# Products of the identity with a bias table: the whole array against two halves of its rows

## The chip, the cores and the metric

The kernel runs on one core of one Trainium2 chip. The metric is the device time of one execution in microseconds (us). Several executions are timed, and one more is profiled; its span and every row below come from that one.

## The reference

A block of attention and a gated feed-forward part, each with a layer norm and a residual, on x of 8 x 256 tokens by 128 features:

```
x = x + layernorm(attention(layernorm(x)))
x = x + layernorm(ffn(x normalised))

attention, 16 heads of 8 features, batches of 256 tokens:
  scores = q k^T / sqrt(8) + rel_bias[clip(i - j + 128, 0, 256)]
  out    = softmax(scores) v, projected by W_out

ffn: h = silu(x w1^T s1) * (x w2^T s2); two layers of 512 x 512 with exact gelu; one of 512 to 128
```

The bias of a head depends only on i - j. So for one head a table of 128 partitions by 384 columns, in which partition p holds the head's bias vector shifted by p, holds all 256 x 256 values: the bias of the second block of 128 rows is the same table, read from another column on.

## The kernel before, in words

**The parts.** The first 31 us load x, normalise it, make the rows of q and k of batch 0 and the maxima of batch 0's scores. Then the attention runs over batches b = 0 to 7, and in each over pairs s = 0 to 7 of two heads (the two heads of a pair are called its halves). From 194 us on the feed-forward part runs, which the change doesn't touch.

**A pair on TensorE.** q and k of a head stand in 33 rows (four parts of 8 that carry the precision, and one row for the maximum or for ones), the first head of a pair on partitions 0 to 32, the second on 64 to 96. In each step of the main loop PE (TensorE) issues, in this order:
- `scores(b, s)`, L1278: 4 products of 33 rows, into one of three two-bank PSUM tiles `place`. The bias was copied into the tile before, by ScalarE (L1023) or VectorE (L699), from the table `raw`; ScalarE then takes the exp (L1016).
- `max_scores(b + 1, s)`, L1244: 4 products of 33 rows, the scores of the next batch, by which their maxima are found.
- `max_bias(b + 1, s)`, L1252: the bias is added to them, by 2 products of the 128 x 128 identity `identr` with 512 columns of `table_hi`, one for each head. VectorE then takes the maxima (L692).
- for pair 7 (`BY_PE`) also `score_bias(b, s)`, L1289: 4 products of the same kind, with `table_hi` and `table_lo`, in place of the copy.
- behind that one other thing: `weighted` (L1304, 16 products with v, four at a time in different columns of the array) behind even pairs, transposes or the output's projection (L1315, L1322, L1261, L1328, L1335) behind odd ones.

A tile `place` is used in turn by scores and by maxima, so exp, products, maxima and bias copy of different pairs wait for each other in a ring of three.

**The tables.** `raw` holds all 16 heads on 128 partitions, 384 columns each, loaded by `load_table` on SP's queue, one pair (384 KB) at a time, among the loads of x. GpSimd copies it into `table_hi` in the rounded format that TensorE takes at full speed (`table_high`, L525), and makes the remainder `table_lo` for pair 7 (L545).

**SP's queue.** The order of SP's transfers is written out by hand: x and tables; then the parts of q and k of unit 1 to DRAM (`store_parts(1)`); a wait until these have landed; eight row loads of batch 1 (`row_dmas(1, ...)`); `load_x(4)`; and then the negated maxima of batch 0, which go from `mrow` into the 33rd rows of q (`send_mrow(sp, 0, 0)`). PE's first `scores(0, 0)` waits for this last transfer, and its first `max_scores(1, 0)` for the row loads.

Of the kernel before, what the change touches and what calls it, by code (L numbers as in the profile page):

```python
# [4 lines left out]
F32 = mybir.dt.float32  # L5
# [9 lines left out]
P = 128  # L15
# [5 lines left out]
REL = 2 * MAX_REL + 1  # L21
WIN = P + S
EXT = WIN + P - 1
CH = 512
NCH = TOK // CH
TPC = CH // P
# [31 lines left out]
BY_PE = (7,)  # L58
BY_DVE = (2, 5)
LAST_BY_DVE = (1, 2, 4, 5, 6)  # L60
LOW_AT_SLOT = {2 * s + k: 2 * i + k for i, s in enumerate(BY_PE) for k in range(2)}


def windows(ap, start, step, count, width):

    return bass.AP(tensor=ap.tensor, offset=ap.offset + start, ap=[list(ap.ap[0]), [step, count], [1, width]])
# [20 lines left out]
def build(nc, x, wq, wk, wv, bqk, brows, bv, wo, bo, ext, w1, s1, w2, s2, h1, h1s, h2, h2s, w3, w3s,  # L87
          ident_in, out):
    ctx = ExitStack()
    with ctx:  # L90
        def sb(name, shape, dt=F32):
            return ctx.enter_context(nc.sbuf_tensor(name, shape, dt))

        def sem(name):
            return ctx.enter_context(nc.semaphore(name))

        ident = sb("ident", [P, P])
        identr = sb("identr", [P, P], F32R)
        wq_sb = sb("wq_sb", [P, D])
        wk_sb = sb("wk_sb", [P, D])  # L100
        wv_sb = sb("wv_sb", [P, D])
# [34 lines left out]
        taken = [qk_parts[0][:, n, :, 0:S] for n in range(2)]  # L136

        raw = sb("raw", [P, H, WIN])
        hi_at, lo_at = 0, H * WIN
        rows_at = lo_at + 2 * len(BY_PE) * WIN  # L140
        room = sb("room", [P, max(rows_at + 4 * PAIRS * S, 2 * NK * CH * SLOTS)], F32R)
        table_hi = room[:, hi_at:lo_at].rearrange("p (h c) -> p h c", h=H)
        table_lo = room[:, lo_at:rows_at].rearrange("p (h c) -> p h c", h=2 * len(BY_PE))
        q_rows = room[:, rows_at:rows_at + 2 * PAIRS * S].rearrange("p (a h n) -> p a h n", a=2, h=PAIRS)
        k_rows = room[:, rows_at + 2 * PAIRS * S:rows_at + 4 * PAIRS * S].rearrange(
            "p (a h n) -> p a h n", a=2, h=PAIRS)
# [55 lines left out]
        def max_tile(i):  # L202
            return place[1 + i % 2 if i < PAIRS else i % 3]

        def score_tile(i):
            return place[i % 3]
# [30 lines left out]
        taken_set = sem("taken_set")  # L237
        row_less = sem("row_less")
        rows_set = sem("rows_set")
        table_hi_pool = sem("table_hi_pool")  # L240
        table_lo_set = sem("table_lo_set")
        dve_order = sem("dve_order")
# [121 lines left out]
        def wait_score_place(eng, i):  # L364

            if i == 0:
                eng.wait_ge(rows_set, 2 * PAIRS)
            elif i == 1:
                eng.wait_ge(ms_read, PAIRS - 1)
            elif i + SHARED < B * PAIRS:  # L370
                eng.wait_ge(ms_read, i + SHARED + 1)
            else:
                eng.wait_ge(exp_done, i - 2)

        def spread_weights(copy, i, halves=range(2)):

            weights = (wq_sb, wk_sb)[i][:, :]
            for half in halves:
# [2 lines left out]
                to = row_w[:, i, :, 64 * half:64 * half + KROWS].rearrange("p s (a d) -> p s a d", a=PARTS)  # L381
                copy(to, src).then_inc(row_w_set[i], 1)

        def load_table(eng, s):
            eng.dma_start(raw[:, 2 * s:2 * s + 2, :],
                          bass.AP(tensor=ext.tensor, offset=2 * s * EXT,
                                  ap=[[1, P], [EXT, 2], [1, WIN]])).then_inc(raw_in[s], 16)
# [9 lines left out]
        def _(sp):  # L397
# [5 lines left out]
            load_x(0)  # L403
            sp.dma_start(ident[:, :], ident_in).then_inc(ident_loaded, 16)
            load_x(1)
            load_table(sp, 0)
            load_x(2)
            load_table(sp, 1)
            load_table(sp, 2)
            sp.wait_ge(ones_set, 2)  # L410
            for half in range(2):
                to = 64 * half + KROWS
                for rows, src in ((q_rows, zeros), (k_rows, ones)):
                    sp.dma_start(rows[to:to + 1, 1, :, :].bitcast(F32), src[0:PAIRS, :].bitcast(F32)).then_inc(extra_in, 16)
            load_table(sp, 3)
            load_table(sp, 4)
            load_x(3)
            for s in range(5, PAIRS):
                load_table(sp, s)

            def store_twice(dram, first, step, src, done):
                plane, row = dram.ap[0][0], dram.ap[1][0]
# [6 lines left out]
            def store_parts(u):  # L429

                first, tiles = UNITS[u]
                tok = slice(first * P, (first + tiles) * P)
                for i, dram in enumerate((q_dram, k_dram)):
                    sp.wait_ge(qk_hi_set, (u - 1) * 2 + i + 1)
                    hi = qk_hi[u][:, i, :].bitcast(F32)
                    if i == 0:
                        sp.dma_start(dram[0, :, tok], hi).then_inc(parts_out[u], 16)
                    else:
                        store_twice(dram[:, :, tok], 0, 2, hi, parts_out[u])
                    sp.wait_ge(qk_lo_set, (u - 1) * 2 + i + 1)  # L440
                    sp.dma_start(dram[1, :, tok], qk_lo[u][:, i, :].bitcast(F32)).then_inc(parts_out[u], 16)
# [22 lines left out]
                row_dmas(b, r * RPAIRS, RPAIRS, rows_in[r][b % 2])  # L464

            store_parts(1)
            sp.wait_ge(parts_out[1], PARTS_OUT)
            row_dmas(1, 0, PAIRS, second_rows_in)
            load_x(4)
# [4 lines left out]
            for b in range(B):  # L474
                send_mrow(sp, b, 1)
                if b == 1:
                    for dst, src in ((hs[:, 0, :], s1), (hs[:, 1, :], s2), (hs[:, 2, :], h1s), (hs[:, 3, :], h2s),
                                     (w3s_sb[:, :], w3s)):
                        sp.dma_start(dst, src).then_inc(scales_in, 16)
                if 1 <= b <= len(matrices):  # L480
                    at, src = matrices[b - 1]
                    sp.dma_start(w_lo[:, at:at + src.shape[-1]], src).then_inc(ffn_w_in[b - 1], 16)
                if b + 2 < B:
                    sp.wait_ge(st_ready, b * PAIRS + RPAIRS)
                    load_rows(b + 2, 0)
                if b == 0:
                    for dst, src in ((wo_sb[:, :], wo), (bo_bc[:, :], bo.broadcast_to((P, D)))):
                        sp.dma_start(dst, src).then_inc(out_w_in, 16)
                    store_parts(3)
                if b + 1 < B:  # L490
                    send_mrow(sp, b + 1, 0)
                if b == 3:
                    store_parts(4)
                if b + 2 < B:
                    sp.wait_ge(st_ready, b * PAIRS + PAIRS)
                    load_rows(b + 2, 1)
# [9 lines left out]
        def _(pool):  # L506
# [14 lines left out]
                inv_std(u + 1, UNITS[u][1], UNITS[u][0])  # L521

            def table_high(s):
                pool.wait_ge(raw_in[s], 16)
                nc.gpsimd.tensor_copy(table_hi[:, 2 * s:2 * s + 2, :],  # L525
                                      raw[:, 2 * s:2 * s + 2, :]).then_inc(table_hi_pool, 1)

            x_inv_std(0)
            pool.wait_ge(qk_w_in[1], 16)
# [10 lines left out]
            pool.wait_ge(xn_set, 4)  # L540
            table_high(6)
            table_high(7)
            for i, s in enumerate(BY_PE):
                pool.wait_ge(table_hi_pool, s + 1)
                nc.gpsimd.tensor_tensor(table_lo[:, 2 * i:2 * i + 2, :], raw[:, 2 * s:2 * s + 2, :],  # L545
                                        table_hi[:, 2 * s:2 * s + 2, :].bitcast(F32),
                                        ALU.subtract).then_inc(table_lo_set, 1)

            x_inv_std(4)
# [60 lines left out]
        def _(dve):  # L610
# [71 lines left out]
            x_normalize(1)  # L682
            dve.wait_ge(qk_w_in[2], 16)
            nc.vector.tensor_scalar(bq_sb[:, 0:1], bq_sb[:, 0:1], scale, None, ALU.mult).then_inc(bq_scaled, 1)
            nc.vector.tensor_copy(identr[:, :], ident[:, :]).then_inc(identr_set, 1)
            x_moments(2)
            q_and_k_low(1, 0)
            q_and_k_low(1, 1)
# [7 lines left out]

            def write_bias(i):
                wait_score_place(dve, i)
                nc.vector.tensor_copy(score_tile(i)[:, :, :].rearrange("p k (j n) -> p k j n", j=2),  # L699
                                      pair_windows(raw[:, :, :], i % PAIRS)).then_inc(bias_set_dve, 1)  # L700

# [232 lines left out]
        def _(act):  # L934
# [85 lines left out]
            def write_bias(i):  # L1020

                wait_score_place(act, i)
                nc.scalar.copy(score_tile(i)[:, :, :].rearrange("p k (j n) -> p k j n", j=2),  # L1023
                               pair_windows(raw[:, :, :], i % PAIRS)).then_inc(bias_set, 1)

# [138 lines left out]
        def _(pe):  # L1164
# [65 lines left out]
            def max_scores(b, s):  # L1230
# [11 lines left out]
                for it in range(TPB):  # L1242
                    for half in range(2):
                        mm(max_tile(b * PAIRS + s)[:, half, it * S:(it + 1) * S],  # L1244
                           rows(q_rows, b, half, s)[:, it * P:(it + 1) * P], rows(k_rows, b, half, s),
                           start=(it == 0), stop=False, skip_group_check=True)

            def max_bias(b, s):
                if b == 0:
                    pe.wait_ge(table_hi_pool, s + 1)  # L1250
                for half in range(2):
                    last = mm(max_tile(b * PAIRS + s)[:, half, :], identr[:, :],  # L1252
                              windows(table_hi[:, 2 * s + half, :], 0, P, 2, S),
                              start=False, stop=True, skip_group_check=True)
                last.then_inc(ms_ready, 1)

            def maxima_T(b, r):
# [26 lines left out]
            def score_bias(b, s):  # L1284
                if b == 0:
                    pe.wait_ge(table_lo_set, BY_PE.index(s) + 1)
                for half in range(2):
                    for part in (table_hi[:, 2 * s + half, :], table_lo[:, LOW_AT_SLOT[2 * s + half], :]):
                        last = mm(score_tile(b * PAIRS + s)[:, half, :], identr[:, :], windows(part, 0, P, 2, S),  # L1289
                                  start=False, stop=True, skip_group_check=True)  # L1290
                last.then_inc(st_ready, 1)

            def weighted(b, g):
# [41 lines left out]
                    last = nc.tensor.transpose(misc[:, it * P:(it + 1) * P], z[:, it, :], ident[:, :])  # L1335
                last.then_inc(zT_ready, 1)

            pe.wait_ge(identr_set, 1)
            for s in range(PAIRS):
                if s + 1 < PAIRS:  # L1340
                    row_lows(s + 1)
# [320 lines left out]
```

## Time and profile before

| | |
|---|---|
| median of 3 runs | 291.06 us (290.31 to 291.15) |
| the profiled execution, its own time | 290.61 us |
| its span | 288.8 us |
| mean granted clock of TensorE | 0.992 |
| attention part | 31 to 194 us of the span |

The span runs from the first to the last instruction, and the time of an execution is 1.8 us longer. In the chain of waits each piece is followed back to what released it. Of products of TensorE the profile gives start and a modelled end; they overlap, so it is the distance between starts that tells the pace.

### The profile page before, as it was taken

Reading aid. Unit: us, or ns where it says so; the run is one execution under the profiler, and the core shown is the slowest. Engines: PE = TensorE matmul, PEld = TensorE weight load, DVE = VectorE, ACT = ScalarE, POOL = GpSimd, SP = SyncE. Lnnn points to the kernel's source line nnn. Section 1 sums busy time; section 2 is a strip of 40 time slices with the busy share of each in tenths; the row PEclk is TensorE's granted clock in tenths of the full one; section 3 lists DMA queues with packets and bytes.
Section 4 is the critical chain, followed back from the end, with each engine's and each line's share of the span. In section 5 each row is a group of like instructions: output and inputs, shape, how many; then the busy total and the mean of one; then the engine's idle time right before and its main releaser. Section 6 shows DMA issues by size and latency. Waiting matters only on the chain.

```text
span 288.8 us, 5174 instructions
## 1 busy us (share of the span) xinstructions
PE 267.7 (93%) x1875; PEld 180.7 (63%) x1875; DVE 212.5 (74%) x442; ACT 205.2 (71%) x316; POOL 102.5 (35%) x107
## 2 busy tenths in 40 slices
PE   7899989899999999999999998999999999999980
PEld 7656646555555555556555554557888888888860
DVE  4576977889789789789788888857654853673675
ACT  2677777785876776785886886767459976896750
POOL 6716000101702603923974985117640202400111
PEclk9999999999999999999999999999999999999996
DMA  6979505322221262560221200000000000010012
GB/s 159 339 231 142 184 5 183 129 65 90 64 84 41 74 194 103 179 210 21 75 78 36 78 0 3 1 3 1 0 2 0 0 0 2 0 36 2 2 36 77
DMA packets 21356, 21.17 MB, mean 73 GB/s; under 512 B 3664, under 2 KB 18768, under 8 KB 21072
## 3 DMA queue, kind: packets, MB, share of 16 engines
q1 hardware_dynamic: 20464, 20.53, 24.4%
q10 hardware_dynamic: 864, 0.27, 0.4%
q8 instruction: 17, 0.28, 0.4%
q14 instruction: 11, 0.09, 0.1%
HBM read 14.90 MB, written 5.64 MB: 71 GB/s over the span
## 4 chain that ended last, share of the span: by engine, by line
PE 68%; DVE 16%; ACT 8%; issue 5%; DMA 1%; POOL 1%; ACTq 0%; POOLq 0%; DVEq 0%
PE place L1449 11%; PE place L1450 11%; PE place L1252 10%; PE pv L1304 7%; DVE mx L692 6%; PE place L1244 5%; ACT ring L1016 4%; PE place L1278 4%; DVE place L699 3%; PE place L1203 2%; PE misc L1315 2%; PE place L1289 2%; PE misc L1182 2%; PE pv L1450 2%; PE pv L1449 2%
## 5 line engine op out<-in xcount | busy, mean ns | idle before, releaser
L692 DVE TENSOR_REDUCE mx<-place 128x4 f32<-128x1024 f32 x64 | 78.3, 1223 | 16.2 <-PE place L1252 14.9
L517 POOL TENSOR_TENSOR rstd<-mv,mhalf 128x2 f32<-128x2 f32 (+1 forms) x26 | 20.9, 806 | 145.8 <-DVE mv L624 145.8
L1016 ACT ACTIVATE ring<-place 128x1024 f32<-128x1024 f32 x64 | 65.7, 1028 | 6.4 <-PE place L1289 3.1
L1252 PE MATMUL place<-room,identr 128*128 128x512 f32 x128 | 47.0, 448 | 0.0
L1023 ACT COPY place<-raw 128x1024 f32<-128x1024 f32 x37 | 37.8, 1024 | 11.7 <-DVE mx L692 11.7
L1449 PE MATMUL place<-room,w_hi 128*128 128x512 f32 (+1 forms) x116 | 44.7, 387 | 0.7 <-DVE room L825 0.7
L1450 PE MATMUL place<-room,w_hi 128*128 128x512 f32 (+1 forms) x116 | 44.1, 383 | 0.0
L1304 PE MATMUL pv<-ring,vx 128*9 128x256 f32 x512 | 33.6, 380 | 0.4 <-ACT ring L1016 0.4
L825 DVE TENSOR_TENSOR room<-ring,room 128x512 fp32r<-128x512 f32 x32 | 21.3, 690 | 17.1 <-ACT room L1104 17.1
L1244 PE MATMUL place<-room 33*128 33x256 f32 x256 | 28.4, 298 | 4.9 <-ACT ring L1016 4.8
L1278 PE MATMUL place<-room 33*128 33x256 f32 x256 | 31.7, 328 | 1.4 <-DVE place L699 1.1
L1278 PEld LDWEIGHTS place<-room 33*128 33x128 f32 x256 | 19.0, 185 | 15.7 <-issue 12.5
L1028 ACT COPY oT<-pv 128x256 f32<-128x256 f32 x32 | 11.8, 370 | 23.2 <-PE pv L1304 23.1
L1244 PEld LDWEIGHTS place<-room 33*128 33x128 f32 x256 | 19.8, 185 | 12.3 <-issue 9.0
L1449 PEld LDWEIGHTS place<-room,w_hi 128*128 128x128 f32 x116 | 21.8, 188 | 5.1 <-DVE room L825 0.9
L1252 PEld LDWEIGHTS place<-room,identr 128*128 128x128 f32 x128 | 19.1, 188 | 8.6
L1450 PEld LDWEIGHTS place<-room,w_hi 128*128 128x128 f32 x116 | 21.8, 188 | 4.1
L699 DVE COPY place<-raw 128x1024 f32<-128x1024 f32 x19 | 23.2, 1225 | 0.6
L1102 ACT ACTIVATE ring<-place,hs 128x512 f32<-128x512 f32 x27 | 18.5, 685 | 5.1 <-PE place L1450 5.1
L1304 PEld LDWEIGHTS pv<-ring,vx 128*9 128x9 f32 x512 | 10.9, 90 | 17.8 <-issue 10.5
L837 DVE SCALAR_TENSOR_TENSOR ring<-place,hs,raw 128x512 f32<-128x512 f32 x16 | 12.0, 750 | 11.9 <-ACT raw L1081 11.6
L1104 ACT CAST room<-ring 128x512 fp32r<-128x512 f32 x32 | 19.9, 621 | 1.0
(141 smaller groups left out, 434.4 us busy)
## 6 DMA issues: line engine op xcount, KB each, us to landing
raw<-ext SPq DMA_DIRECT2D x8, 384.0 KB, 6.8
room<-q_parts SPq DMA_DIRECT2D x48, 64.0 KB
room<-k_parts SPq DMA_DIRECT2D x48, 64.0 KB
w_lo<-h SPq DMA_DIRECT2D x2, 1024.0 KB, 5.6
q_parts<-w_hi SPq DMA_DIRECT2D x4, 256.0 KB, 3.0
k_parts<-w_hi SPq DMA_DIRECT2D x2, 512.0 KB, 3.4
xs<-x SPq DMA_DIRECT2D x3, 256.0 KB, 6.1
w_lo<-w SPq DMA_DIRECT2D x3, 256.0 KB, 2.8
```

Source lines behind the costliest of these rows:

```text
L517: nc.gpsimd.tensor_tensor(rstd[:, at:at + width], mv[:, at:at + width, 1], mhalf[:, 0:width], ALU.pow).then_inc(rstd_set, 1)
L692: nc.vector.tensor_reduce(mx[:, s // RPAIRS, :, :, s % RPAIRS].rearrange("p i k -> p k i"), max_tile(b * PAIRS + s)[:, :, :].rearrange("p ...
L699: nc.vector.tensor_copy(score_tile(i)[:, :, :].rearrange("p k (j n) -> p k j n", j=2), pair_windows(raw[:, :, :], i % PAIRS)).then_inc(bia ...
L825: nc.vector.tensor_tensor(lo, act_f[:, half[c], k, :], hi.bitcast(F32), ALU.subtract).then_inc((a1_lo_set, a2_lo_set)[i], 1)
L1016: nc.scalar.activation(probs[:, s % PRING, :, :, :].rearrange("p k j n -> p (k j n)"), score_tile(b * PAIRS + s)[:, :, :].rearrange("p k n ...
L1023: nc.scalar.copy(score_tile(i)[:, :, :].rearrange("p k (j n) -> p k j n", j=2), pair_windows(raw[:, :, :], i % PAIRS)).then_inc(bias_set, 1)
L1244: mm(max_tile(b * PAIRS + s)[:, half, it * S:(it + 1) * S], rows(q_rows, b, half, s)[:, it * P:(it + 1) * P], rows(k_rows, b, half, s), st ...
L1252: last = mm(max_tile(b * PAIRS + s)[:, half, :], identr[:, :], windows(table_hi[:, 2 * s + half, :], 0, P, 2, S), start=False, stop=True, ...
L1278: last = mm(tile[:, half, j * S:(j + 1) * S], rows(k_rows, b, half, s)[:, j * P:(j + 1) * P], rows(q_rows, b, half, s), start=(s in BY_PE ...
L1304: last = mm(pv[32 * r:32 * r + VC, 0:S], vx[:, b * TPB + j, 4 * g + r, :], probs[:, (2 * g + r // 2) % PRING, r % 2, j, :], start=(j == 0) ...
L1449: mm(o, w, hi, start=first, stop=False)
L1450: done = mm(o, w, lo, start=False, stop=last and exact)
```

## The change

A head's table is held on 64 partitions in place of 128, with 448 columns in place of 384: the first head of a pair on partitions 0 to 63, the second on 64 to 127, as the rows of q and k are. A product of the identity then takes 64 rows of the array. Output rows 0 to 63 of a block come from the table at column 0, output rows 64 to 127 from column 64. For the first the weights are [I, 0], for the second [0, I], both read from one tile `ident_wide` of 192 columns, 0 I 0. Per pair `max_bias` now has 4 products (two column blocks times two heads), and `score_bias` 8.

The half tables are loaded first, in place of the whole ones, into space of `w_lo` (`raw_halves`), 16 transfers of 112 KB. The whole tables `raw`, which the bias copies still read, are loaded by SP behind `store_parts(1)`. ScalarE and VectorE wait for them in `write_bias`. SP waits for `table_hi` and `table_lo` ahead of the weight load at b = 1, whose place is that of the half tables.

```diff
+HP = P // 2
+TWIN = WIN + HP
...
+        def load_halves(eng, s):
+
+            for half in range(2):
+                eng.dma_start(raw_halves[half * HP:(half + 1) * HP, s, :],
+                              bass.AP(tensor=ext.tensor, offset=(2 * s + half) * EXT,
+                                      ap=[[1, HP], [1, TWIN]])).then_inc(table_in[s], 16)
...
-            load_table(sp, 0)
+            load_halves(sp, 0)
             load_x(2)
-            load_table(sp, 1)
-            load_table(sp, 2)
+            load_halves(sp, 1)
+            load_halves(sp, 2)
...
-            load_table(sp, 3)
-            load_table(sp, 4)
+            load_halves(sp, 3)
+            load_halves(sp, 4)
             load_x(3)
             for s in range(5, PAIRS):
-                load_table(sp, s)
+                load_halves(sp, s)
...
             store_parts(1)
+            for s in range(PAIRS):
+                load_table(sp, s)
             sp.wait_ge(parts_out[1], PARTS_OUT)
             row_dmas(1, 0, PAIRS, second_rows_in)
             load_x(4)
...
             def table_high(s):
-                pool.wait_ge(raw_in[s], 16)
-                nc.gpsimd.tensor_copy(table_hi[:, 2 * s:2 * s + 2, :],
-                                      raw[:, 2 * s:2 * s + 2, :]).then_inc(table_hi_pool, 1)
+                pool.wait_ge(table_in[s], 32)
+                nc.gpsimd.tensor_copy(table_hi[:, s, :], raw_halves[:, s, :]).then_inc(table_hi_pool, 1)
...
-            nc.vector.tensor_copy(identr[:, :], ident[:, :]).then_inc(identr_set, 1)
+            dve.wait_ge(blank_set, 1)
+            nc.vector.tensor_copy(ident_wide[:, 0:2 * HP], blank[:, :]).then_inc(identr_set, 1)
+            nc.vector.tensor_copy(ident_wide[:, 2 * HP:3 * HP], blank[:, 0:HP]).then_inc(identr_set, 1)
+            dve.wait_ge(identr_set, 1)
+            for half in range(2):
+                at = half * HP
+                nc.vector.tensor_copy(ident_wide[at:at + HP, HP:2 * HP],
+                                      ident[at:at + HP, at:at + HP]).then_inc(identr_set, 1)
...
             def write_bias(i):
                 wait_score_place(dve, i)
+                dve.wait_ge(raw_in[i % PAIRS], 16)
...
+            def bias_product(tile, table, s, block, half):
+
+                at = half * HP
+                return mm(tile[:, half, :], ident_wide[at:at + HP, HP - block * HP:3 * HP - block * HP],
+                          windows(table[at:at + HP, s, :], block * HP, P, 2, S), start=False, stop=True,
+                          skip_group_check=True)
+
             def max_bias(b, s):
                 if b == 0:
                     pe.wait_ge(table_hi_pool, s + 1)
-                for half in range(2):
-                    last = mm(max_tile(b * PAIRS + s)[:, half, :], identr[:, :],
-                              windows(table_hi[:, 2 * s + half, :], 0, P, 2, S),
-                              start=False, stop=True, skip_group_check=True)
+                for block in range(2):
+                    for half in range(2):
+                        last = bias_product(max_tile(b * PAIRS + s), table_hi, s, block, half)
                 last.then_inc(ms_ready, 1)
```

## Rows read from the trace of the kernel before

**Rows 1.** The page: busy time by engine; transfers in 40 equal slices.

```profile
PE 267.7 (93%) x1875; PEld 180.7 (63%) x1875; DVE 212.5 (74%) x442; ACT 205.2 (71%) x316; POOL 102.5 (35%) x107
...
GB/s 159 339 231 142 184 5 183 129 65 90 64 84 41 74 194 103 179 210 21 75 78 36 78 0 3 1 3 1 0 2 0 0 0 2 0 36 2 2 36 77
```

**Rows 2.** The page: the chain that ended last, by engine and by line.

```profile
PE 68%; DVE 16%; ACT 8%; issue 5%; DMA 1%; POOL 1%; ACTq 0%; POOLq 0%; DVEq 0%
PE place L1449 11%; PE place L1450 11%; PE place L1252 10%; PE pv L1304 7%; DVE mx L692 6%; PE place L1244 5%; ACT ring L1016 4%; PE place L1278 4%; DVE place L699 3%; PE place L1203 2%; PE misc L1315 2%; PE place L1289 2%; PE misc L1182 2%; PE pv L1450 2%; PE pv L1449 2%
```

**Rows 3.** The chain of waits in time, 83 to 126 us: start, us, what.

```profile
94.00 0.95 PE place L1289 x4
...
99.28 0.66 PE place L1252 x2
99.94 0.44 PE misc L1315 x4
...
102.69 0.59 PE misc L1315 x4
...
103.95 0.68 PE place L1252 x2
```

**Rows 4.** Busy time by engine, PEclk, DMA share and GB/s, a batch.

```profile
82.90:104.00 21.10, 20.02 (x171) 11.58 (x172) 17.80 (x32) 15.50 (x23) 6.10 (x6) 1.00 0.27 74
```

**Rows 5.** The chain of waits, 142 to 176 us, shares by line.

```profile
by line: DVE mx L692 21.2%; ACT ring L1016 13.6%; issue 11.5%; PE pv L1304 8.7%; PE place L1252 8.6%; DVE stats L616 5.9%; ACT place L1023 5.6%; PE place L1244 5.1%; PE misc L1328 3.9%; DVE y_and_z L627 3.1%; DVE mv L620 3.0%; DVE y_and_z L
```

**Rows 6.** PE's instructions in order of time, narrow windows: start, us, what.

```profile
103.43 0.28 PE L1278 MATMUL place<-room 33*128 33x256 f32 x2
...
103.67 0.28 PE L1244 MATMUL place<-room 33*128 33x256 f32 x2
103.88 0.50 PE L1252 MATMUL place<-room,identr 128*128 128x512 f32 x1
...
106.25 0.40 PE L1252 MATMUL place<-room,identr 128*128 128x512 f32 x1
106.58 0.41 PE L1304 MATMUL pv<-ring,vx 128*9 128x256 f32 x4
```

**Rows 7.** The same of the first part: VectorE, then weight loads.

```profile
9.55 0.21 DVE L685 CAST identr<-ident 128x128 fp32r<-128x128 f32 x1
...
13.09 0.88 DVE L647 SCALAR_TENSOR_TENSOR z_parts<-place,bq_sb,z_parts 128x256 fp32r<-128x256 f32 x2 [1.93 <-ACT z_parts L954]
...
20.27 0.19 PEld L1210 LDWEIGHTS place<-z_parts,minus_ident 128*128 128x128 f32 x1 [0.45 <-ACT z_parts L967]
```

**Rows 8.** The same, SP's queue: issue time and its length.

```profile
8.84 1.76 SPq L385 DMA_DIRECT2D raw<-ext  x3
...
14.46 0.49 SPq L441 DMA_DIRECT2D k_parts<-z_parts  x1
...
22.86 1.69 SPq L401 DMA_DIRECT2D xs<-x  x1
```

**Rows 9.** Busy time of stretches; the last two columns are DMA share and GB/s.

```profile
14.00:16.00 2.00, 1.99 (x10) 1.20 (x10) 0.65 (x1) 1.39 (x4) 1.00 (x2) 1.00 1.06 370
...
18.00:20.00 2.00, 2.00 (x11) 1.26 (x10) 1.40 (x2) 1.64 (x4) 0.00 (x0) 1.00 0.12 40
...
22.00:28.00 6.00, 6.00 (x33) 4.05 (x32) 4.32 (x13) 4.50 (x11) 3.70 (x4) 1.00 1.17 138
```

**Rows 10.** DMA issues at 22.0 to 22.5, then at 22.8 us: KB, us to landing.

```profile
room<-k_parts SPq DMA_DIRECT2D x2, 128.0 KB, 6.7
...
xs<-x SPq DMA_DIRECT2D x1, 256.0 KB, 7.1
```

**Rows 11.** PE's instructions in order of time, 32 to 35 us.

```profile
33.30 0.51 PE L1278 MATMUL place<-room 33*128 33x256 f32 x4
```

**Rows 12.** The last PE work; then busy time and, third from the end, PEclk.

```profile
280.79 0.78 PE L1542 MATMUL place<-ident,xT 128*128 128x128 f32 x4 [0.42 <-ACT xT L1118]
...
284.00:286.00 2.00, 0.00 (x0) 0.00 (x0) 1.58 (x5) 0.00 (x0) 0.20 (x1) 0.58 0.24 71
```

More of the change, by code:

```diff
@@ L60 @@
 LAST_BY_DVE = (1, 2, 4, 5, 6)
-LOW_AT_SLOT = {2 * s + k: 2 * i + k for i, s in enumerate(BY_PE) for k in range(2)}
+LOW_PAIRS = BY_PE
 def windows(ap, start, step, count, width):
@@ L97, in build @@
         ident = sb("ident", [P, P])
-        identr = sb("identr", [P, P], F32R)
         wq_sb = sb("wq_sb", [P, D])
@@ L138, in build @@
         raw = sb("raw", [P, H, WIN])
[L139 to L143, printed above, removed]
+        hi_at, lo_at = 0, PAIRS * TWIN
+        rows_at = lo_at + len(LOW_PAIRS) * TWIN
+        ident_at = rows_at + 4 * PAIRS * S
+        room = sb("room", [P, max(ident_at + 3 * HP, 2 * NK * CH * SLOTS)], F32R)
+        raw_halves = w_lo[:, 2 * PAIRS * P:2 * PAIRS * P + PAIRS * TWIN].rearrange("p (s c) -> p s c", s=PAIRS)
+        table_hi = room[:, hi_at:lo_at].rearrange("p (s c) -> p s c", s=PAIRS)
+        table_lo = room[:, lo_at:rows_at].rearrange("p (s c) -> p s c", s=len(LOW_PAIRS)) if LOW_PAIRS else None
+        ident_wide = room[:, ident_at:ident_at + 3 * HP]
         q_rows = room[:, rows_at:rows_at + 2 * PAIRS * S].rearrange("p (a h n) -> p a h n", a=2, h=PAIRS)
@@ L239, in build @@
         rows_set = sem("rows_set")
+        table_in = [sem(f"table_in{s}") for s in range(PAIRS)]
         table_hi_pool = sem("table_hi_pool")
@@ L479, in _ @@
                         sp.dma_start(dst, src).then_inc(scales_in, 16)
+                if b == 1:
+                    sp.wait_ge(table_hi_pool, PAIRS)
+                    sp.wait_ge(table_lo_set, len(LOW_PAIRS))
                 if 1 <= b <= len(matrices):
@@ L542, in _ @@
             table_high(7)
-            for i, s in enumerate(BY_PE):
+            for i, s in enumerate(LOW_PAIRS):
                 pool.wait_ge(table_hi_pool, s + 1)
-                nc.gpsimd.tensor_tensor(table_lo[:, 2 * i:2 * i + 2, :], raw[:, 2 * s:2 * s + 2, :],
-                                        table_hi[:, 2 * s:2 * s + 2, :].bitcast(F32),
+                nc.gpsimd.tensor_tensor(table_lo[:, i, :], raw_halves[:, s, :], table_hi[:, s, :].bitcast(F32),
                                         ALU.subtract).then_inc(table_lo_set, 1)
@@ L1022, in write_bias @@
                 wait_score_place(act, i)
+                act.wait_ge(raw_in[i % PAIRS], 16)
                 nc.scalar.copy(score_tile(i)[:, :, :].rearrange("p k (j n) -> p k j n", j=2),
@@ L1286, in score_bias @@
                     pe.wait_ge(table_lo_set, BY_PE.index(s) + 1)
[L1287 to L1290, printed above, removed]
+                for table, at in ((table_hi, s), (table_lo, LOW_PAIRS.index(s))):
+                    for block in range(2):
+                        for half in range(2):
+                            last = bias_product(score_tile(b * PAIRS + s), table, at, block, half)
                 last.then_inc(st_ready, 1)
@@ L1336, in norm_T @@
                 last.then_inc(zT_ready, 1)
-            pe.wait_ge(identr_set, 1)
+            pe.wait_ge(identr_set, 4)
             for s in range(PAIRS):
```

## The prediction

> **What bounds the kernel now.** I read the page's busy shares first. TensorE (PE) is busy 93% of the span, VectorE 74%, ScalarE 71%, and the core's transfers are dense only in the first slices [rows 1]. The chain that ended last is 68% PE and 16% VectorE, and the products of the identity with the table, L1252, hold 10% of it [rows 2]. One batch of the attention part, read from the chain in order of time (82.9 to 104 us), is a nearly closed row of PE work: scores L1278, scores for the maxima L1244, table product L1252, then a product or transpose [rows 3]. So a saving in PE's sequence is worth its face value there, as long as VectorE (17.8 us busy of that batch's 21.1) and ScalarE (15.5) don't take over [rows 4]. From 142 us on, long stretches of the chain are VectorE and ScalarE [rows 5]. The FFN part, from 194 us, is not touched.
>
> **The edit on PE.** max_bias goes from 2 products of 128 rows and 512 columns to 4 of 64 rows and 512 columns, score_bias from 4 to 8. Do two of the new ones run at once, on the two halves of the rows? The score products answer: they use partitions 0 to 32 and 64 to 96, and from their pair at 103.43 to the next but one at 103.67 it is two steps of 0.12 us, and both products of a pair lie inside the same 0.28 us [rows 6]. A pair of 512 columns should then go at the pace of one now, 0.23 us (an L1289 product, 0.95 us for four [rows 3]). Two pairs cost what two products cost: 0.46 us. The streaming time neither gains nor loses. The other end, no overlap, costs 2 x 0.23 us for each of 64 pairs: +29 us.
>
> What goes is the step from half-row products to full-row products. The last L1244 pair starts at 103.67 and needs 0.12 us; L1252 starts only at 103.88, and its first product takes 0.50 us where a second takes 0.40, since it waits 0.10 us for its weights [rows 6]. 103.88 + 0.10 - 103.79 = 0.19, call it 0.20 us for each table product. In the new form its weights can load under the running score products, as those of L1244 do under L1278.
>
> The page "TensorEngine Tiling (Array Packing)" of the Trainium skill, section Key Properties, says that changing the tiling mode drains TensorE. The gap before L1252 agrees. By the same rule the drain returns where a full-row transpose follows the table product, so by it the 6 places counted at 0.05 us below would fall to 0 and the sum to 6.4 us.
>
> The rows say how much returns. Four L1315 transposes cost 0.44 us in the chain behind L1252 but 0.59 behind the pv products, which use the array in another shape [rows 3]: 0.15 us comes back, 0.05 us is left. Behind a table product followed by pv products there is a change of shape already now (L1304 starts 0.33 us after the last L1252 product, whose columns need 0.23 [rows 6]), so nothing comes back: 0.20. Where VectorE, or ScalarE by way of L1289, is released by the product, its end is what counts: 0.20.
>
> In the batch of rows 3 that is 3 to pv, 1 to L1289, 1 to VectorE (the last) at 0.20, and 1 to L1315 at 0.05: 1.05 us. Over the chain from 31 to 190 us I count 32 places at 0.20 and 6 at 0.05 (batches as in rows 3 three times; from 142 us only five): 6.4 + 0.3 = 6.7 us. From it I take 0.7 off for VectorE, which would be 89% busy in a batch of 20.0 us. **6.0 us** saved; bounds 3 (every place where VectorE or ScalarE is next lost) and 7.
>
> **Edits at nothing.** Ahead of 31 us PE waits for ScalarE in each pair, 0.45 us ahead of L1210 [rows 7]: the product's 0.2 us is hidden there. GpSimd's table copies shrink from 768 to 448 columns, and GpSimd has 1% of the chain now [rows 2], so they can only be earlier. VectorE's 0.21 us cast of the identity becomes four copies, at most 4 x 0.21, that is 0.6 us more ahead of an idle time of 1.93 us [rows 7]; without that cover it would be 0.6 us. The new waits on raw_in in write_bias cost nothing if the tables land ahead of the first scores at 33.3 us; behind them ScalarE's and VectorE's queues would hold the first exp and maxima. The wait ahead of the weight load at b = 1 is long met.
>
> **The DMA queue is the price.** SP issues 16 half loads for 8 whole ones: 8 x 0.47 = 3.8 us more, so the last goes out at 14.4 instead of 10.6, and store_parts(1) starts 1.3 us late, ending at 16.2 instead of 14.95 [rows 8]. The bytes there fall (8 x 384 KB to 16 x 112 KB). Then the 8 whole tables, 3.15 MB, are issued, 8 x 0.49 = 3.9 us, to 20.1. The stores, issued from 14.4 to 16.2 into a queue that the smaller halves have left, have landed by then, so row_dmas(1), load_x(4) and send_mrow(0,0) are all issued behind the tables. With tables in it the full queue moves 370 GB/s at most [rows 9], 339 in a whole slice [rows 1]; I take 350: 3.15 / 0.35 = 9.0 us. I allow 2 us from the first issue to the first bytes (in rows 8 and 9, from the last stores at 14.46 and the idle slice behind them, it is not more than some 4), so they hold the engines from 18.2 to 27.2. Now that time is idle at 18 to 20, and the row loads run at 138 GB/s with the engines full (share 1.17) from 20.0 on; the last, issued at 22.4, lands at 22.4 + 6.7 = 29.1, load_x(4) at 22.86 + 7.1 = 30.0 [rows 8 to 10]. That is 9.1 to 10 us of work, moved behind the tables: 27.2 + 9.1 to 10 = 36.3 to 37.2. The mrow copy follows. The first scores(0,0) waits for it, and starts now at 33.3 [rows 11]; behind it on PE stand max_scores(1,0) and with it VectorE's next maxima. A stall of 3.0 to 3.9 us; I take **3.5**. Lower bound 0 (rows at the tables' rate: 27.2 + 1.31 / 0.35 = 31); upper bound: tables at the row loads' 138 GB/s, 23 us, a landing near 51 and a stall of 17. The rows with table loads in them are the 339 to 370, so I stay near it. That nothing overtakes is read from load_x(4), which lands 0.9 us behind the row load ahead of it though it was issued into the same crowd. What is late next, mrow(0,1), is needed four pairs later and is not in danger.
>
> **Sum.** -6.0 + 3.5 = -2.5 us on the profiled execution: 290.61 - 2.5 = 288.1 (span 288.8 to 286.3, 1.8 us around it). The median of the runs is 0.45 above the profiled one: 291.06 - 2.5 = 288.5 us.
>
> **Rivals.**
> A. The clock falls in the stall. PE would be idle 3.5 us with nothing to do. At the end of the kernel the last PE work starts at 280.79 and ends near 281.6, and the granted clock of 284 to 286 is 0.58, which puts the fall to half near 284.3 [rows 12]: 2.7 us after it. Against: gaps there were frequent before that too. If the slow stretch lasts some 4 us and PE is two thirds of the chain, it loses about 1.5: 290.0. The page "TensorE: Matmul & The Clock Gate" (Part 1) of the Trainium skill says that idleness puts the clock to half; it is the same case, and it gives 290.0 too.
> B. No stall: the tables and the rows overlap, or mrow gets in ahead. For: the engines are nearly idle at 18 to 20. Against: share above 1 at only 138 GB/s [rows 9]. 291.06 - 6.0 = 285.0.
> C. Gain given back: each 0.2 us on PE turns into a wait for VectorE's maxima or ScalarE's bias copy (VectorE is 84% busy in rows 4 and leads in rows 5). 3 us saved, 3.5 lost: 291.5, no change.
> D. Slower: the tables go at 230 GB/s (the mean of a slice with mixed loads [rows 1]) or worse; 13.7 us, the mrow copy lands at 41.5, stall 8.2: 291.06 - 6.0 + 8.2 = 293.3. It decides from a landing at 39.3 on. For: everything is one queue. Against: rows 9.
> E. The halves don't overlap at 512 columns: +29 - 6 + 3.5, near 318. Against: rows 6.
>
> **Chances.** Forecast 0.43 (own range 287.3 to 289.8), A 0.20, B 0.12, C 0.10, D 0.12, E 0.03. Range 284.8 to 292.5: E, most of D and the edge of B are left out. A change under 0.3% (0.9 us) can't be told from none. Faster (below 290.2): 0.41 + 0.11 of A + 0.12 of B = 0.64. Same: 0.02 + 0.07 of A + 0.07 of C = 0.16. Slower: 0.20.
>
> **What would show it.** Right: LDWEIGHTS of the table product start while L1244's products run, its first product starts 0.12 us after the last of them, two of its products in the same time, pv starting about 0.2 us sooner; transposes behind it cost 0.15 more; batches of 20.1 instead of 21.1 us. SP's table loads at 16 to 20 us, DMA full to 37, PE idle 33 to 37 for a DMA into room. Wrong: products in single file, batches of 21 us, no idle PE at 33 us, or a clock below 1.00 behind it.

## The result

The changed kernel takes 293.91 us (median of 6 runs, 292.66 to 294.81), against 290.96 us before (6 runs): a ratio of 1.0099, 95% interval 1.0082 to 1.0117. Forecast were 288.5 us, in a range of 284.8 to 292.5. The kernel is slower, by 2.95 us, and the time lies outside the range.

The profiled execution took 293.98 us, its span is 292.2. The page shows two things that it doesn't show before: PE is busy less (263.7 us against 267.7), and the granted clock has a hole in slices 6 and 7 of 40, counted from 1.

```profile
PE 263.7 (90%) x2035; PEld 177.0 (61%) x2035; DVE 212.8 (73%) x445; ACT 205.2 (70%) x316; POOL 100.0 (34%) x107
...
PEclk9999956999999999999999999999999999999996
...
GB/s 175 144 234 363 196 183 3 130 172 75 85 74 101 11 76 221 190 114 174 47 92 48 76 0 3 3 2 0 2 0 0 0 2 0 0 40 0 0 36 76
...
PE 58%; DVE 16%; SPq 9%; ACT 7%; issue 6%; DMA 3%; POOL 0%; ACTq 0%; DVEq 0%
```

The dense transfers have moved from slice 2 to slice 4 against [rows 1], and SP's queue and a DMA hold 12% of a chain in which they had 1% [rows 2]. The waits of PE name the DMA:

```profile
PE place L1313 <- DMA room<-mrow: 6.3, 2, 6.0
PE place L1273 <- ACT ring L1044: 4.3, 12, 0.4
```

PE in order of time, around the first scores(0,0) (now L1313; L1273 are the scores for the maxima, L1280 all products of the identity):

```profile
31.76 1.16 PE L1217 MATMUL pv<-wv_sb,ring 128*128 128x128 f32 x8
38.88 0.80 PE L1313 MATMUL place<-room 33*128 33x256 f32 x4 [5.96 <-DMA room<-mrow]
39.48 0.63 PE L1273 MATMUL place<-room 33*128 33x256 f32 x4
39.91 1.05 PE L1280 MATMUL place<-room 64*128 64x512 f32 x4
```

scores(0,0) starts at 38.88, not at 33.30 [rows 11]. It takes 0.80 us, not 0.51, at a granted clock of 0.50 in place of 1.00. The busy times in stretches show when (third column from the end is the clock):

```profile
32.00:34.00 2.00, 0.92 (x8) 0.73 (x7) 2.00 (x3) 1.42 (x2) 0.00 (x0) 1.00 1.15 191
34.00:36.00 2.00, 0.00 (x0) 0.00 (x0) 0.27 (x1) 0.00 (x0) 0.00 (x0) 0.80 1.19 191
36.00:38.00 2.00, 0.00 (x0) 0.00 (x0) 0.00 (x0) 0.00 (x0) 0.00 (x0) 0.50 1.08 322
...
46.00:48.00 2.00, 2.00 (x20) 0.44 (x16) 1.23 (x1) 1.02 (x2) 0.00 (x0) 0.50 0.00 0
48.00:50.00 2.00, 2.00 (x12) 0.89 (x10) 0.00 (x0) 0.28 (x1) 0.00 (x0) 0.78 0.00 0
```

PE ends its work at 32.9. If the granted clock is either full or half, as wherever it holds for a whole stretch here, 0.80 over 34 to 36 puts the fall at 35.2, and 0.78 over 48 to 50 the rise at 48.9, ten microseconds after PE took up work again.

Behind that hole the kernel is as forecast. A batch takes 20.1 us where it took 21.1 [rows 4], with VectorE 17.70 us busy of it:

```profile
90.20:110.30 20.10, 19.03 (x191) 10.82 (x192) 17.70 (x33) 15.53 (x23) 6.10 (x6) 1.00 0.21 59
```

One pair of it, from its scores to the transposes behind the table product, PE in order of time (the last line is the next pair's first products):

```profile
104.58 0.50 PE L1313 MATMUL place<-room 33*128 33x256 f32 x4
104.92 0.40 PE L1273 MATMUL place<-room 33*128 33x256 f32 x4
105.16 0.63 PE L1280 MATMUL place<-room 64*128 64x512 f32 x4
105.72 0.66 PE L1350 MATMUL misc<-ident,oT 128*128 128x128 f32 x4
106.30 0.39 PE L1313 MATMUL place<-room 33*128 33x256 f32 x2
```

The same place in the kernel before:

```profile
103.55 0.40 PE L1244 MATMUL place<-room 33*128 33x256 f32 x4
103.88 0.74 PE L1252 MATMUL place<-room,identr 128*128 128x512 f32 x2
```

L1280 starts 0.24 us after L1273, where L1252 started 0.33 after L1244 and then waited 0.10 for its weights [rows 6]. Four products take 0.63 us, where two took 0.74. The weights of L1280 now load while L1273 still runs (first line), and in the chain of waits a table product takes 0.47 us (0.66 to 0.68 in [rows 3]) and the four transposes behind it 0.59:

```profile
105.04 0.31 PEld L1280 LDWEIGHTS place<-room 64*128 64x128 f32 x4
...
105.32 0.47 PE place L1280 x4
105.79 0.59 PE misc L1350 x4
```

### The profile page after: what moved, and what is told of

Same layout as the page of the kernel before. It is cut to its first block, busy times and chain, and to the rows that moved or that the text cites. A ratio compares the mean times of both kernels' runs of the same rounds, so it can differ in the third digit from the quotient of the medians.

```text
span 292.2 us, 5568 instructions
## 1 busy us (share of the span) xinstructions
PE 263.7 (90%) x2035; PEld 177.0 (61%) x2035; DVE 212.8 (73%) x445; ACT 205.2 (70%) x316; POOL 100.0 (34%) x107
## 4 chain that ended last, share of the span: by engine, by line
PE 58%; DVE 16%; SPq 9%; ACT 7%; issue 6%; DMA 3%; POOL 0%; ACTq 0%; DVEq 0%
PE place L1484 11%; PE place L1485 10%; PE place L1280 8%; PE pv L1339 7%; DVE mx L719 7%; PE place L1313 4%; PE place L1273 4%; ACT ring L1044 4%; DVE place L727 4%; SPq L396 3%; DMA room<-mrow 3%; PE misc L1350 2%; SPq L468 2%; PE misc L1211 2%; PE pv L1485 2%
## 5 line engine op out<-in xcount | busy, mean ns | idle before, releaser
L1280 PE MATMUL place<-room 64*128 64x512 f32 x320 | 49.6, 401 | 0.0
L1313 PE MATMUL place<-room 33*128 33x256 f32 x256 | 32.6, 336 | 7.0 <-DMA room<-mrow 6.3
L1339 PE MATMUL pv<-ring,vx 128*9 128x256 f32 x512 | 34.5, 388 | 0.5 <-ACT ring L1044 0.5
L853 DVE TENSOR_TENSOR room<-ring,room 128x512 fp32r<-128x512 f32 x32 | 21.3, 689 | 17.1 <-ACT room L1133 17.1
L1273 PE MATMUL place<-room 33*128 33x256 f32 x256 | 29.2, 305 | 4.6 <-ACT ring L1044 4.3
L1313 PEld LDWEIGHTS place<-room 33*128 33x128 f32 x256 | 19.6, 190 | 21.9 <-issue 13.2
L1273 PEld LDWEIGHTS place<-room 33*128 33x128 f32 x256 | 20.5, 192 | 12.0 <-issue 8.6
L1280 PEld LDWEIGHTS place<-room 64*128 64x128 f32 x320 | 27.0, 192 | 1.2
L727 DVE COPY place<-raw 128x1024 f32<-128x1024 f32 x19 | 23.2, 1225 | 0.6
```

The source lines that it names most:

```text
L853: nc.vector.tensor_tensor(lo, act_f[:, half[c], k, :], hi.bitcast(F32), ALU.subtract).then_inc((a1_lo_set, a2_lo_set)[i], 1)
L1273: mm(max_tile(b * PAIRS + s)[:, half, it * S:(it + 1) * S], rows(q_rows, b, half, s)[:, it * P:(it + 1) * P], rows(k_rows, b, half, s), st ...
L1280: return mm(tile[:, half, :], ident_wide[at:at + HP, HP - block * HP:3 * HP - block * HP], windows(table[at:at + HP, s, :], block * HP, P, ...
L1313: last = mm(tile[:, half, j * S:(j + 1) * S], rows(k_rows, b, half, s)[:, j * P:(j + 1) * P], rows(q_rows, b, half, s), start=(s in BY_PE ...
L1339: last = mm(pv[32 * r:32 * r + VC, 0:S], vx[:, b * TPB + j, 4 * g + r, :], probs[:, (2 * g + r // 2) % PRING, r % 2, j, :], start=(j == 0) ...
```

## The experiments

All times are medians beside runs of the kernel before on the same chip: 290.85 us in the first set, 290.95 in the second, 290.88 in the third. The theory: the half-row products gain over 6 us; the whole tables ahead of the row loads hold up the first maxima rows by 5.6 us; and the idle time that this makes brings the clock down, for over 3 us more. The rivals: the clock falls because of the half-row products themselves; or the products gain little.

**halves_only**, the products alone.

```diff
--- the kernel before
             def max_bias(b, s):
...
-                for half in range(2):
-                    last = mm(max_tile(b * PAIRS + s)[:, half, :], identr[:, :],
-                              windows(table_hi[:, 2 * s + half, :], 0, P, 2, S),
-                              start=False, stop=True, skip_group_check=True)
+                for block in range(2):
+                    for half in range(2):
+                        last = bias_product(max_tile(b * PAIRS + s), table_hi, 2 * s + half, block, half)
```

bias_product takes rows 64 half to 64 half + 63 of identr and of the whole table; score_bias is split in the same way. Both products of a head are then the same one: half of the output rows get the bias twice and the other half none. The sizes and the number of products are those of the changed kernel.

> The kernel before with its loads and its whole tables, and only the products of the identity split into 64 rows each (twice as many). It adds the bias of the wrong columns to the rows, so part of the result is not the reference's; the work is that of the changed kernel. Theory: each table product ends 0.2 us sooner, batches of 20.1 us, no stall, clock 1.00; 285.0 us. Rival (half-row products gain little, the gain in the changed kernel came from shifted waits): 289 to 291 us.

Measured: 284.14 us (284.01 to 284.37), ratio 0.9769 (0.9753 to 0.9786). The products are worth 6.7 us, and they are no cause of a falling clock: it stays at 1.00. scores(0,0) starts at 33.01, and a batch takes what it takes in the changed kernel; the rows are of PE in order of time and of the busy times in stretches:

```profile
33.01 0.50 PE L1283 MATMUL place<-room 33*128 33x256 f32 x4
```

```profile
73.80:93.90 20.10, 19.02 (x194) 10.82 (x196) 17.71 (x33) 15.54 (x24) 7.07 (x7) 1.00 0.23 68
```

**loads_only**, the loads alone.

```diff
--- the changed kernel
-                for block in range(2):
-                    for half in range(2):
-                        last = bias_product(max_tile(b * PAIRS + s), table_hi, s, block, half)
+                for half in range(2):
+                    last = bias_product(max_tile(b * PAIRS + s), table_hi, s, half)
```

bias_product is here one product of 128 rows, with `ident_wide[:, 0:P]`.

> The changed kernel with its loads and their order, but two full-row products per pair as before (over the half tables read as whole ones, so the bias values are wrong). Theory: stall of 5.6 us and half clock behind it, batches of 21.1 us as before; 291.0 + 5.6 + 3.3 = 299.9 us. Rival (the stall is partly hidden when PE has more to do): 296 us or less.

Measured: 300.81 us (300.43 to 301.7), ratio 1.0335 (1.0317 to 1.0354), 10.0 us slower. The two parts nearly add up: 10.0 - 6.7 = 3.3 us, and the whole change measures 2.95. They are not quite the same parts, since here scores(0,0) starts 5.0 us later than before (38.27 against 33.30), not 5.6, and the low clock lasts longer, from 37.5 to 54.6 us. In its trace, PE in order of time shows the stall, and the busy times in stretches show the clock and a batch of 21.1 us:

```profile
38.27 0.80 PE L1310 MATMUL place<-room 33*128 33x256 f32 x4 [4.57 <-DMA room<-mrow]
```

```profile
34.00:38.00 4.00, 0.00 (x0) 0.00 (x0) 1.03 (x2) 0.00 (x0) 0.00 (x0) 0.94 1.14 258
38.00:48.00 10.00, 9.73 (x52) 5.86 (x52) 4.91 (x4) 4.87 (x6) 0.00 (x0) 0.50 0.22 83
48.00:52.00 4.00, 4.00 (x15) 1.93 (x12) 0.75 (x1) 1.61 (x3) 0.00 (x0) 0.50 0.00 0
...
54.00:56.00 2.00, 2.00 (x19) 1.11 (x22) 2.00 (x3) 1.60 (x2) 0.00 (x0) 0.85 0.48 146
...
87.00:108.10 21.10, 20.01 (x175) 11.59 (x178) 17.80 (x32) 15.52 (x23) 6.86 (x8) 1.00 0.23 65
```

**fill**, the clock alone.

```diff
--- the changed kernel
+            pe.wait_ge(ms_read, PAIRS)
+            stream(place[2][:, 0, :], blank, blank, 44)
             for b in range(B):
                 more = b + 1 < B
```

> The changed kernel with 44 products of a zero tile put ahead of the first scores(0,0), where TensorE stands idle for 5.96 us and the granted clock falls to half from 35 to 49 us. Theory (price is the late maxima rows plus the fallen clock): the rows still land at 38.8 us, but the clock stays at 1.00 and scores(0,0) to scores(0,3) takes 7.5 us again instead of 10.7; 290.6 us. Rival (the clock falls because the products use half the rows, or for another reason): the clock still falls, 294 us.

Measured: 290.07 us (289.43 to 294.56 in 10 runs), ratio 0.9981 (0.9963 to 0.9999). Little of the stall is gone: scores(0,0) starts at 38.62, as the zero products end. But the clock is full. Against the kernel before on its own chip, fill is 0.78 us faster and the changed kernel 2.95 us slower, so 3.7 us come back. The traces agree: from scores(0,0) to scores(0,3) it is 7.0 us here (38.62 to 45.66) and 10.7 in the changed kernel (38.88 to 49.62). So this much was the clock's. What is left, a stall of 5.3 us against the products' 6.7, would make -1.4; measured is -0.8. (In one of the ten, 294.56 us, the clock fell all the same, by its mean of 0.979.) PE in order of time, then the same scores(0,3) in the changed kernel:

```profile
33.07 5.54 PE L1199 MATMUL place<-blank 128*128 128x256 f32 x44
38.62 0.50 PE L1313 MATMUL place<-room 33*128 33x256 f32 x4
...
45.66 0.50 PE L1313 MATMUL place<-room 33*128 33x256 f32 x4
```

```profile
49.62 0.50 PE L1313 MATMUL place<-room 33*128 33x256 f32 x4
```

The ten microseconds behind the stall in fill, at a clock of 1.00:

```profile
39.00:49.00 10.00, 8.97 (x82) 4.75 (x80) 7.23 (x7) 8.20 (x11) 0.00 (x0) 1.00 0.14 51
```

**fill_half**, the same with 22 products.

```diff
--- fill
-            stream(place[2][:, 0, :], blank, blank, 44)
+            stream(place[2][:, 0, :], blank, blank, 22)
```

> The changed kernel with 22 products of the zero tile ahead of the first scores(0,0) in place of the 44 of the earlier run, so that TensorE is idle some 3 us and not 5.96. Theory (any idle stretch of about 3 us brings the clock down, as the last one of the kernel before did after 2.7 us): the clock falls again, 293 to 294 us. Rival (only a longer one does): clock 1.00 and 290.1 us.

Measured: 293.73 us (292.64 to 294.28), ratio 1.0083 (1.0057 to 1.0108). PE idles 3.34 us, and nearly all of the clock's price is paid again, 3.6 us against fill (2.78 us slower than before, where fill was 0.78 faster):

```profile
33.23 2.88 PE L1199 MATMUL place<-blank 128*128 128x256 f32 x22
39.45 0.80 PE L1313 MATMUL place<-room 33*128 33x256 f32 x4 [3.34 <-DMA room<-mrow]
```

**late_tables**, the order of the loads.

```diff
--- the changed kernel
             store_parts(1)
-            for s in range(PAIRS):
+            for s in range(2):
                 load_table(sp, s)
...
             send_mrow(sp, 0, 0)
+            for s in range(2, PAIRS):
+                if s not in BY_PE:
+                    load_table(sp, s)
             store_parts(2)
```

> The changed kernel with only the whole tables of pairs 0 and 1 ahead of the row loads; those of pairs 2 to 6 go out behind the first transfer of maxima, that of pair 7 is left out, since nothing reads it. Theory: the first maxima rows land near 33 us, stall of at most 1 us, the clock stays at 1.00; 285.5 to 286.5 us. Rival (the tables come too late for the bias copies of pairs 2 and 3, which become the wait): 289 us or more.

Measured: 284.29 us (283.94 to 284.65), ratio 0.9776 (0.9759 to 0.9793). This version beats both kernels. scores(0,0) starts at 32.94 without a wait. The rival's wait is no longer than it was: 0.60 us for the bias copy of scores(0,2), 0.66 in the kernel before:

```profile
32.94 0.50 PE L1316 MATMUL place<-room 33*128 33x256 f32 x4
...
36.86 0.50 PE L1316 MATMUL place<-room 33*128 33x256 f32 x4 [0.60 <-DVE place L730]
```

**five_ahead**, the dose: five whole tables ahead, pairs 5 and 6 behind the first maxima.

```diff
--- late_tables
-            for s in range(2):
+            for s in range(5):
...
-            for s in range(2, PAIRS):
+            for s in range(5, PAIRS):
```

> The changed kernel with five whole tables ahead of the row loads in place of eight, pairs 5 and 6 behind the first maxima, pair 7 left out. Theory (each table of 384 KB ahead of the row loads is 1.1 us of stall once the queue is full): stall of 5.6 - 3.4 = 2.2 us; 284.3 + 2.2 = 286.5 us with the clock at 1.00, about 289.5 if it falls. Rival (the stall is a threshold matter, not proportional): 284.3 or 293.9 us.

Measured: 288.6 us (285.17 to 289.38), ratio 0.9891 (0.9819 to 0.9963). scores(0,0) at 35.10: three tables fewer are 3.8 us, 1.26 each. In the profiled run an idle time of 2.04 us was enough for the clock. Three of the four runs are alike (288.4 to 289.4 us, mean clock 0.98); the fourth, at 0.991, took 285.17. That is less than late_tables and this trace's stall make at full clock (284.3 + 2.2 = 286.5 us), so its stall was probably shorter too; no trace of it shows this. In the profiled one the clock falls after PE has been at work again for over a microsecond (0.94 of 35 to 37 puts the fall at 36.8), and rises at 43.6:

```profile
35.10 0.50 PE L1316 MATMUL place<-room 33*128 33x256 f32 x4 [2.04 <-DMA room<-mrow]
```

```profile
35.00:37.00 2.00, 1.90 (x20) 1.31 (x22) 0.65 (x1) 1.36 (x2) 0.00 (x0) 0.94 1.08 388
37.00:43.00 6.00, 6.00 (x42) 3.24 (x40) 4.16 (x4) 3.53 (x5) 0.00 (x0) 0.50 0.45 169
43.00:45.00 2.00, 2.00 (x14) 0.98 (x12) 0.00 (x0) 0.43 (x1) 0.00 (x0) 0.85 0.00 0
```

**one_issue and late_one_issue**, both half tables of a pair in one transfer. They were to show what SP's 16 issues cost. GpSimd waits for one transfer of a pair in place of two.

```diff
--- the changed kernel; the same to late_tables
-            for half in range(2):
-                eng.dma_start(raw_halves[half * HP:(half + 1) * HP, s, :],
-                              bass.AP(tensor=ext.tensor, offset=(2 * s + half) * EXT,
-                                      ap=[[1, HP], [1, TWIN]])).then_inc(table_in[s], 16)
+            eng.dma_start(raw_halves[:, s, :],
+                          bass.AP(tensor=ext.tensor, offset=2 * s * EXT,
+                                  ap=[[EXT, 2], [1, HP], [1, TWIN]])).then_inc(table_in[s], 16)
...
```

> The changed kernel with both half tables of a pair in one transfer, 8 issues in place of 16; all 8 whole tables still ahead of the row loads. Theory (2 us of the 5.6 us stall are SP's issues, which the prediction put at 0.47 us each and which took 0.61): the first scores(0,0) at 36.5 to 37 us instead of 38.9, a stall near the predicted 3.5; 291.9 us if the clock still falls for its whole low stretch, 288.5 if it doesn't. Rival (the stall is set by the bytes alone): scores(0,0) at 38.5 or later, 293.9 us.

> Two whole tables ahead, five behind the first maxima (as in late_tables, 284.3 us), and both half tables of a pair in one transfer. Theory: with no stall left, 8 fewer issues on SP change nothing, since TensorE waits for ScalarE's rows until 31 us; 284.3 us. Rival (the start still hangs on the loads): 283 us.

Measured: 319.04 us (317.59 to 320.23), ratio 1.0967, and 313.27 us, ratio 1.0773. Both theories missed; the edit did something else. While these loads run, the 16 DMA engines are busy 0.14 of the time and move 51 GB/s, and SP's issues take up to several microseconds (busy times of 8 to 20 us, then SP's queue in order of time):

```profile
8.00:20.00 12.00, 10.28 (x58) 7.00 (x56) 7.56 (x27) 9.11 (x21) 2.54 (x4) 1.00 0.14 51
```

```profile
3.43 4.76 SPq L395 DMA_DIRECT2D w_lo<-ext  x2
8.23 3.84 SPq L429 DMA_DIRECT2D room<-zeros  x1
```

0.14 is little over two engines' share of sixteen, and the outermost dimension of the source counts two. The Trainium skill, "DMA: Bandwidth & Descriptors", section "Why a DMA increments its semaphore by 16 and not by 1", says that the number of engines is the largest one up to 16 that divides the slowest dimension of both sides: here 2. The trace agrees.

**grouped**, 8 issues again, but over 64 partitions: pairs 0; 1, 2; 3, 4; 5 to 7, each group in one transfer per half.

```diff
--- the changed kernel
-        def load_halves(eng, s):
+        def load_halves(eng, s, n):
...
-                eng.dma_start(raw_halves[half * HP:(half + 1) * HP, s, :],
+                eng.dma_start(raw_halves[half * HP:(half + 1) * HP, s:s + n, :],
                               bass.AP(tensor=ext.tensor, offset=(2 * s + half) * EXT,
-                                      ap=[[1, HP], [1, TWIN]])).then_inc(table_in[s], 16)
+                                      ap=[[1, HP], [2 * EXT, n], [1, TWIN]])).then_inc(table_in[s], 16)
...
```

> The changed kernel with the half tables in groups of 1, 2, 2 and 3 pairs, each group in 2 transfers over 64 partitions, so 8 issues in place of 16 without the two-row outer dimension that made one_issue slow; all 8 whole tables still ahead of the row loads. Theory (2 us of the 5.6 us stall come from SP's issues): the first scores(0,0) at 36.5 to 37.2 us instead of 38.9; the clock falls all the same, 291.5 to 292.5 us. Rival (bytes alone set it): 38.5 us or later, 293.9 us.

Measured: 289.67 us (285.01 to 290.69), some 2 us below what was expected; the ratio, 0.9869 (0.9787 to 0.9951), rests on the runs of 285.01 and 289.13 us alone. scores(0,0) starts at 35.98, 2.9 us sooner than in the changed kernel: the issues of SP were about half of the stall. By the mean clocks (0.975 to 0.980) the clock fell in three of the four runs; the fourth, at 0.991, took 285.01, which is 2.9 us less than grouped_fill below takes at full clock, and the later start there explains only 1.0 of it. So not only its clock but its stall was probably another. SP's queue shows how the time is saved. In the changed kernel the last three pairs' half tables are issued from 12.62 to 16.33 and the whole tables from 18.49; here the whole tables go from 14.96. First the changed kernel, then grouped:

```profile
12.62 3.71 SPq L396 DMA_DIRECT2D w_lo<-ext  x6
16.36 0.58 SPq L453 DMA_DIRECT2D q_parts<-z_parts  x1
...
18.49 4.70 SPq L401 DMA_DIRECT2D raw<-ext  x8
```

```profile
13.01 0.35 SPq L450 DMA_DIRECT2D q_parts<-z_parts  x1
...
14.96 5.13 SPq L401 DMA_DIRECT2D raw<-ext  x8
```

**grouped_fill**, grouped with 26 products of the zero tile ahead of scores(0,0).

```diff
--- grouped
+            pe.wait_ge(ms_read, PAIRS)
+            stream(place[2][:, 0, :], blank, blank, 26)
```

> As grouped, and 26 products of the zero tile ahead of the first scores(0,0). This is the case that the prediction took: a stall of 3.5 us and the clock at 1.00. Theory: 284.3 + 3.5 = 287.8 us. Rival (the stall is 5.6 and the filler ends too early, so the clock falls): 293 us.

Measured: 287.96 us (287.55 to 288.11), ratio 0.9895 (0.9878 to 0.9911). scores(0,0) at 36.99, as the zero products end, and with no wait for the maxima: the start is set by them here, a microsecond later than in grouped. So this run says nothing more on SP's issues, but it is the forecast's own case, PE held up by 3.7 us (36.99 against 33.30) at full clock, and it takes the forecast's time: 2.9 us less than the kernel before, where 2.5 were forecast.

```profile
33.69 3.37 PE L1196 MATMUL place<-blank 128*128 128x256 f32 x26
36.99 0.50 PE L1310 MATMUL place<-room 33*128 33x256 f32 x4
```

**late_grouped**, late_tables with the grouped half tables (both edits above).

> late_tables (284.3 us) with the grouped half tables. Theory: no stall is left and TensorE waits for ScalarE's rows until 31 us, so 8 fewer issues change nothing; 284.3 us. Rival (SP's queue still sets the first scores): 283.3 us or less.

Measured: 284.26 us (284.12 to 284.59), ratio 0.9771 (0.9754 to 0.9787). Once nothing stalls at 33 us, SP's issues cost nothing.

## Why the prediction was wrong

**What bounds the kernel, and the edit on PE: right, slightly undersized.** The count over the chain gave 6.7 us, from which 0.7 was taken off for VectorE; halves_only measures 6.7 (6.2 to 7.2 by its interval). VectorE was 17.7 us busy in a batch of 20.1 (88%) and took nothing back. The terms show in the trace: no gap ahead of the table products, 0.47 us in the chain for two pairs of half-row products where 0.46 was forecast, and 0.59 us for four transposes behind a table product, where it was 0.44 [rows 3]. Rivals C and E are refuted. B is too, since the stall is there.

**The edits at nothing: right.** Up to 31 us the changed kernel is 0.3 us ahead (its last table product of that part starts at 31.11, before at 31.45), and no write_bias waits for raw.

**The DMA queue: right mechanism, wrong size, 5.6 us for 3.5.** The term that failed is SP's issues. The prediction had 16 half loads at 0.47 us, with the stores out by 16.2 and the tables issued from there to 20.1. They take 0.61 each on average (the last six from 12.62 to 16.33), so the stores are out at 18.45 and the tables at 23.2. That is 2.3 us later at the tables' start, and the first scores come 2 us later than forecast. While the halves were issued the DMA engines had little to do: 0.22 busy from 8 to 10 us, where it was 1.04 before. The other terms held in sum. The tables went at 379 to 384 GB/s from 24 to 28 us, where 350 was taken, and the maxima landed some 9.3 us after that rate had ended, near 29.6, where 9.1 to 10 was taken; the row loads alone went faster than their 138, at 169 to 191. Rival D, whose 293.3 us lies next to the result, has the wrong mechanism: its tables go at 230 GB/s.

Busy times of the changed kernel (the last columns are DMA share and GB/s):

```profile
8.00:10.00 2.00, 1.58 (x8) 1.10 (x7) 1.59 (x8) 1.02 (x2) 1.42 (x3) 1.00 0.22 63
...
26.00:28.00 2.00, 2.00 (x14) 1.29 (x12) 0.27 (x1) 1.53 (x4) 1.13 (x1) 1.00 1.06 379
...
30.00:32.00 2.00, 1.98 (x12) 0.79 (x12) 1.92 (x3) 1.12 (x2) 0.00 (x0) 1.00 1.15 169
```

**The clock: the step that decided, and it was only a rival.** The sum had it at nothing; rival A had a chance of 0.20 and a price of 1.5 us, from a low stretch guessed at 4 us. Its mechanism was right and its price wrong. By the mean clocks (0.969 to 0.974) the fall came in all six runs; it lasted 13.7 us in the profiled one, and cost 3.7 us by fill. No row of the kernel before shows how long a low stretch lasts once PE works again, and the 4 us had none behind them. A wide price should have followed, and a chance of one half or more, because the only idle time of that length in the trace, the one at the end [rows 12], had brought the clock down.

So in place of -6.0 + 3.5 = -2.5 us the sum is -6.7 + 5.6 + 3.7 = +2.6 us; the runs show +2.95, and scatter by more than the rest (292.66 to 294.81). Neither error alone leaves the range: with the clock kept up the changed kernel takes 290.07 us (fill), and with fewer issues and the clock fallen in most runs 289.67 (grouped).

What stays open: how long a stall the clock forgives. 2.04 us were too much in the one run of five_ahead that has a trace. How long the stall was in the runs at 285.17 and 285.01 us, in which the clock stayed up, isn't shown.

## What to carry to other kernels

Products that fill half of the array's rows and run in pairs cost no more than full ones, and next to other half-row products they save the change between the two shapes: 0.2 us each here. A load that nobody needs for a while belongs behind the small transfer that everybody waits for, as long as it still lands before it is needed (the tables of pairs 2 to 6 did): on one queue each 384 KB ahead of it cost 1.26 us. And price an idle time of TensorE such as those here (2.0 to 6.0 us) at its own length plus the low clock behind it, which cost 3.7 us after the longest and 3.6 after 3.3 us of idling. Where such a stall can't be taken away, products of zeros in it may keep the clock up; here that was worth 3.7 us.

## What the runs showed of the hardware

- The low clock outlasts its cause. After 6 us of idling it stayed for ten more microseconds of work (35.2 to 48.9 us in the changed kernel). After 2.04 us in five_ahead it lasted 6.8 us in all, and began over a microsecond after work had been taken up again.
- How long the low clock lasts isn't set by the idle time alone: 17.1 us after 4.57 us of idling in loads_only (37.5 to 54.6 us), 13.7 us after 5.96 in the changed kernel. With it the same loads cost 10.0 us in loads_only against 5.6 + 3.7.
- A transfer whose source has an outermost dimension of 2 ran at 51 GB/s on two engines' worth, and SP stood behind it (4.76 us for two issues).
